# A Perceiver layer in fp32: Qk's last 64 channels on quarters of the PE array, weights issued by SP, the first group's q products in one slot, more filler products at the end

## The reference, cut to what matters

```python
def layer(x, ctx):                       # x (128, 32, 256), ctx (128, 257, 192)
    h = layernorm(x)
    q = (h @ Wq).heads(8, 64); k = (ctx @ Wk).heads(8, 64); v = (ctx @ Wv).heads(8, 64)
    x = x + softmax(q @ k.T * 64**-0.5) @ v @ Wo + bo          # cross attention
    h = layernorm(x) * ln_g + ln_b
    w = sigmoid(h @ Wx @ Ww + bw); k, v, r = h @ Wk2, h @ Wv2, sigmoid(h @ Wr2)
    # 4 heads of 64, over 32 steps: state = (1 - w) * state + k v^T;  out = r^T state
    x = x + out @ Wo2
    h = layernorm(x)
    return x + gelu(h @ U1 @ V1 + b1) @ U2 @ V2 + b2
```

## Time and profile before

| | before |
|---|---|
| median of 3 runs | 1028.94 us (1028.15 to 1028.95) |
| the profiled execution, its own time | 1036.5 us |
| its span | 1034.7 us |
| PE busy | 996.9 us, 96% of the span |
| ACT busy | 594.6 us, 57% |
| DVE busy | 503.5 us, 49% |
| POOL busy | 205.8 us, 20% |
| DMA | 79.03 MB, mean 76 GB/s |

### The profile page before, as it was taken

How to read it: one execution, slowest core, us unless ns; L and a number is a source line. 1 busy time by engine, 2 the same in 40 slices (tenths; PEclk the granted TensorE clock), 3 DMA queues, 4 the chain that set the end, 5 groups by cost and what they waited for, 6 DMA issues and landing times.

```text
span 1034.7 us, 21348 instructions
## 1 busy us (share of the span) xinstructions
PE 996.9 (96%) x8318; PEld 806.6 (78%) x8318; DVE 503.5 (49%) x1156; ACT 594.6 (57%) x1418; POOL 205.8 (20%) x356
## 2 busy tenths in 40 slices
PE   3799999999999999999999999999999999999987
PEld 3477888787888878788887878888887888887775
DVE  4444546363554536355453735545373554436152
ACT  2354637557574755758475675847467584746331
POOL 0010303113040312204031220403122040313130
PEclk9899999999999999999999999999999999999799
DMA  8233221222322222232212222222222322212000
GB/s 283 62 98 96 85 83 56 73 75 76 93 69 90 56 78 70 76 93 72 86 57 82 66 76 92 78 82 61 78 66 76 93 72 77 66 63 66 1 11 21
DMA packets 58002, 79.03 MB, mean 76 GB/s; under 512 B 10288, under 2 KB 39856, under 8 KB 57904
## 3 DMA queue, kind: packets, MB, share of 16 engines
q1 hardware_dynamic: 54304, 72.71, 23.2%
q10 hardware_dynamic: 3600, 4.96, 1.4%
HBM read 73.18 MB, written 4.46 MB: 75 GB/s over the span
## 4 chain that ended last, share of the span: by engine, by line
PE 66%; DVE 13%; ACT 12%; issue 4%; POOL 2%; ACTq 1%; SPq 1%; DMA 0%; POOLq 0%; DVEq 0%
PE gb L324 12%; PE scores L369 8%; PE scores L372 6%; PE gb L431 6%; PE gb L491 5%; PE acc L398 5%; PE ptp L381 4%; PE acc L394 4%; DVE inv L837 3%; PE acc L399 3%; ACT probs L603 3%; PE gb L540 3%; DVE probs L747 2%; ACT hid L668 2%; DVE nmax L740 2%
## 5 line engine op out<-in xcount | busy, mean ns | idle before, releaser
L603 ACT ACTIVATE probs<-scores,nmax 128x257 f32<-128x257 f32 x256 | 119.2, 472 | 171.4 <-DVE nmax L740 171.2
L740 DVE TENSOR_REDUCE nmax<-scores 128x2 f32<-128x514 f32 x128 | 88.6, 692 | 226.0 <-PE scores L372 226.0
L933 POOL TENSOR_TENSOR ptm<-probs,head 128x32 f32<-128x32 f32 x128 | 33.1, 259 | 601.9 <-DVE probs L747 601.9
L369 PE MATMUL scores<-raw_t,qk 128*128 128x257 f32 x512 | 134.0, 385 | 1.7 <-ACT qk L638 1.2
L369 PEld LDWEIGHTS scores<-raw_t,qk 128*128 128x128 f32 x512 | 88.1, 192 | 9.4 <-issue 1.6
L372 PE MATMUL scores<-raw_t,qk 64*128 64x257 f32 x512 | 91.2, 433 | 0.0
L747 DVE TENSOR_TENSOR probs<-probs,rinv 128x514 f32<-128x514 f32 x128 | 88.9, 695 | 4.4
L398 PE MATMUL acc<-pt,raw_n 128*128 128x256 f32 x256 | 90.0, 433 | 0.0
L381 PE MATMUL ptp<-ident,probs 128*128 128x128 f32 x512 | 79.0, 277 | 8.1 <-DVE probs L747 6.8
L394 PEld LDWEIGHTS acc<-pt,raw_n 128*64 128x64 f32 x1024 | 56.0, 137 | 37.0 <-issue 28.6
L394 PE MATMUL acc<-pt,raw_n 128*64 128x128 f32 x1024 | 83.5, 284 | 1.1 <-ACT pt L608 1.1
(11 more groups left out here) (140 smaller groups left out, 2356.8 us busy)
## 6 DMA issues: line engine op xcount, KB each, us to landing
raw_t<-in_ctx_t SPq DMA_DIRECT2D x128, 258.0 KB, 2.9
raw_n<-in_ctx_n SPq DMA_DIRECT2D x128, 192.0 KB, 2.4
xin<-in_x SPq DMA_DIRECT2D x16, 256.0 KB, 2.8
xb<-in_x SPq DMA_DIRECT2D x16, 256.0 KB, 2.8
vsp<-tail_values SPq DMA_DIRECT2D x256, 2.0 KB
out<-ob SPq DMA_DIRECT2D x16, 256.0 KB, 2.2
qk<-in_wq ACTq DMA_DIRECT2D x1, 512.0 KB, 4.5
wk<-in_wk SPq DMA_DIRECT2D x1, 512.0 KB, 5.4
```

The costliest lines, as they stand in the source:

```text
L369: mm(scores[:, r, 0:L], w[:, 0, b, r * P:(r + 1) * P], x[:, 0, 0:L], start=True, stop=False)
L603: go(probs[n % 2][:, r, 0:L], scores[:, r, 0:L], ACT.Exp, bias=nmax[:, r:r + 1], accum_out=rsum[:, r:r + 1]).then_inc(s["exp_ready"], 1)
L740: v_.tensor_reduce(nmax[:], scores[:, :, 0:L], AX.X, ALU.max, negate=True)\
```

## The change

**Qk.** `qk_wide(j, g)` (steps Qa0, Qa1) makes channels 0-127 of four heads (pairs p = j and j + 2) with four products of 64 rows and 128 columns of the array. `qk_rest(g)` (step Qb) makes channels 128-191 of all eight heads with eight products on 64 x 64 quarters of the array, into two banks. So a group has three Qk steps and six copies by ACT. `wk` is no longer padded (384 KB instead of 512). `qk` is 384 columns for each batch.

**Slots.** Qa0 in slot 3, Qa1 in slot 5, Qb in slot 6, none in slot 4; q2 and q1 change places (slots 2 and 3), and q3 goes from slot 5 to slot 4. Group 0 has its own table `BEGINNING`, with the four q steps in slot 2.

**The start.** The fifteen weight loads are issued by SP, ahead of the context tiles of batches 1 and 2. ACT does an Exp of two columns behind its small loads, waits for `xn0` and issues the load of x of group 1 itself. POOL waits for the weights only in `residual(0)`. The raw copy of wq is kept in `khat` instead of `qk[1]`, so DVE clears `khat` only after wq is split.

**The end.** `BUSY` has 5 fillers instead of 2 after XT2 of the last group, and 3 instead of 1 after its O2.

```diff
-FILL1 = [["Sq", "Qf", "WV"], ["O2"], [], ["Qk0"], ["Qk2"], ["Qk4", "H0"], ["Qk6"], ["Sp", "H2"]]
-FILL2 = [[], ["Y3", "Y1", "XT"], ["q0", "q1", "Y2", "XT2"], ["z", "q2", "XT3"], ["k", "Pf"], ["q3", "r"], ["v"],
+FILL1 = [["Sq", "Qf", "WV"], ["O2"], [], ["Qa0"], [], ["Qa1", "H0"], ["Qb"], ["Sp", "H2"]]
+FILL2 = [[], ["Y3", "Y1", "XT"], ["q0", "q2", "Y2", "XT2"], ["z", "q1", "XT3"], ["q3", "k", "Pf"], ["r"], ["v"],
          ["TP"]]
+BEGINNING = {1: ["XT"], 2: ["q0", "q2", "q1", "q3"], 3: ["Qa0"], 5: ["Qa1"], 6: ["Qb"]}
-BUSY = {("Y2", OLD): 4, ("XT2", NEXT): 2, ("H2", OLD): 2, ("Y3", OLD): 1, ("O2", NEXT): 1, ("Y2", NEXT): 9,
+BUSY = {("Y2", OLD): 4, ("XT2", NEXT): 5, ("H2", OLD): 2, ("Y3", OLD): 1, ("O2", NEXT): 3, ("Y2", NEXT): 9,
         ("XT3", NEXT): 1, ("Pf", NEXT): 1, ("H2", NEXT): 3, ("Qf", NEXT): 1}
...
+    if i == FIRST:
+        return [[(n, 0) for n in BEGINNING.get(b, [])], []]
...
-        wk = sb("wk", [P, 4, 256])
+        wk = sb("wk", [P, 4, C])
-        qk = [sb(f"qk{i}", [P, 2, G, 256]) for i in range(2)]
+        qk = [sb(f"qk{i}", [P, G, 256 + P]) for i in range(2)]
...
             load_t(0)
             load_n(0)
+            for dst, src in WEIGHTS:
+                sp.dma_start(dst, src).then_inc(wb_in, 16)
             for n in range(1, RING):
                 load_t(n)
                 load_n(n)
-            load_x(1)
             load_x(2)
...
+            def qk_wide(j, g):
+                even, odd = tile(f"Qa{j}e", g), tile(f"Qa{j}o", g)
+                drained(f"q{j}", g)
+                drained(f"q{j + 2}", g)
...
+                for k in range(2):
+                    p = j + 2 * k
+                    last_even = mm(even[:, k], wk[0:64, p, 0:P], qs[0:64, p], start=True, stop=True)
+                    last_odd = mm(odd[:, k], wk[64:128, p, 0:P], qs[64:128, p], start=True, stop=True)
...
+            def qk_rest(g):
+                even, odd = tile("Qbe", g), tile("Qbo", g)
+                for j in range(2):
+                    for k in range(2):
+                        p, half = j + 2 * k, slice(64 * k, 64 * k + 64)
+                        last_even = mm(even[half, j], wk[0:64, p, P:C], qs[0:64, p], start=True, stop=True)
+                        last_odd = mm(odd[half, j], wk[64:128, p, P:C], qs[64:128, p], start=True, stop=True)
...
-                    mm(scores[:, r, 0:L], w[:, 0, b, r * P:(r + 1) * P], x[:, 0, 0:L], start=True, stop=False)
+                    mm(scores[:, r, 0:L], w[:, b, r * P:(r + 1) * P], x[:, 0, 0:L], start=True, stop=False)
...
-                    mm(scores[:, r, 0:L], w[half, 1, b, r * P:(r + 1) * P], x[half, 1, 0:L], start=False,
+                    mm(scores[:, r, 0:L], w[half, b, 2 * P:3 * P], x[half, 1, 0:L], start=False,
...
-            for dst, src in WEIGHTS:
-                act.dma_start(dst, src).then_inc(wb_in, 16)
+            act.wait_ge(s["half_ready"], 1)
+            go(warm[:], half[:], ACT.Exp)
+            act.wait_ge(s["xn0_ready"], 1)
+            act.dma_start(xin[:], x_v[1]).then_inc(x_in, 16)
...
             def constants():
+                dve.wait_ge(s["wq_ready"], 1)
...
             def residual(g):
+                if g == 0:
+                    pool.wait_ge(wb_in, W_B)
...
             pool.wait_ge(small_in, W_S)
-            pool.wait_ge(wb_in, W_B)
```

More of the change, by code:

```diff
@@ L52 @@
           (NG + 1, 7): [("H2", NEXT), ("Qf", NEXT), ("Y3", NEXT)]}
-BUSY = {("Y2", OLD): 4, ("XT2", NEXT): 2, ("H2", OLD): 2, ("Y3", OLD): 1, ("O2", NEXT): 1, ("Y2", NEXT): 9,
+BEGINNING = {1: ["XT"], 2: ["q0", "q2", "q1", "q3"], 3: ["Qa0"], 5: ["Qa1"], 6: ["Qb"]}
+BUSY = {("Y2", OLD): 4, ("XT2", NEXT): 5, ("H2", OLD): 2, ("Y3", OLD): 1, ("O2", NEXT): 3, ("Y2", NEXT): 9,
         ("XT3", NEXT): 1, ("Pf", NEXT): 1, ("H2", NEXT): 3, ("Qf", NEXT): 1}
 TILES = {"WV": ["WV0", "WV1"]}
-for pair in ("Qk0 Qk1", "Qk2 Qk3", "Qk4 Qk5", "Qk6 Qk7", "H0 H1", "H2 H3"):
+for pair in ("H0 H1", "H2 H3"):
     TILES[pair.split()[0]] = pair.split()
+TILES.update({n: [n + "e", n + "o"] for n in ("Qa0", "Qa1", "Qb")})
 TILES.update({"Sp": ["S0", "S1"], "Sq": ["S2", "S3"]})
@@ L61 @@
 SHIFT.update({f"q{p}": PREP for p in range(4)})
-SHIFT.update({f"Qk{h}": PREP for h in range(H)})
+SHIFT.update({n: PREP for n in ("Qa0", "Qa1", "Qb")})
 SHIFT.update({n: POST for n in "WV Y1 XT2 z k r v Sp".split()})
@@ L166, in build @@
         ve, rstd, half = sb("ve", [P, 3, 2]), sb("rstd", [P, 3, 2]), sb("half", [P, 2])
+        warm = sb("warm", [P, 2])
         o_h, o_l = (sb(n, [P, 4, T], F32R) for n in ("o_h", "o_l"))
@@ L345, in q @@
                 done(f"q{p}", g, last)
[L347 to L351, removed]
-                    pe.wait_ge(wk_in, 16)
[L353 to L357, removed]
-                done(f"Qk{h + 1}", g, last_odd)
+            def qk_wide(j, g):
+                even, odd = tile(f"Qa{j}e", g), tile(f"Qa{j}o", g)
+                drained(f"q{j}", g)
+                drained(f"q{j + 2}", g)
+                if g == 0 and j == 0:
+                    pe.wait_ge(wk_in, 16)
+                for k in range(2):
+                    p = j + 2 * k
+                    last_even = mm(even[:, k], wk[0:64, p, 0:P], qs[0:64, p], start=True, stop=True)
+                    last_odd = mm(odd[:, k], wk[64:128, p, 0:P], qs[64:128, p], start=True, stop=True)
+                done(f"Qa{j}e", g, last_even)
+                done(f"Qa{j}o", g, last_odd)
+            def qk_rest(g):
[5 more added lines that the diff above has]
+                        last_odd = mm(odd[half, j], wk[64:128, p, P:C], qs[64:128, p], start=True, stop=True)
+                done("Qbe", g, last_even)
+                done("Qbo", g, last_odd)
             def score(n):
@@ L363, in score @@
                 if b == 0:
-                    drained("Qk7", g)
+                    drained("Qbo", g)
                 if n > 0:
@@ L557, in _ @@
                 steps[f"q{i}"] = lambda g, i=i: q(i, g)
-                steps[f"Qk{2 * i}"] = lambda g, i=i: qk_heads(2 * i, g)
             steps["Sp"], steps["Sq"] = lambda g: s_tiles(0, g), lambda g: s_tiles(1, g)
+            for j in range(2):
+                steps[f"Qa{j}"] = lambda g, j=j: qk_wide(j, g)
+            steps["Qb"] = qk_rest
             for i in (0, 2):
@@ L1062 @@
     wk = np.asarray(L0_xattn_Wk).T.reshape(H // 2, P, C).transpose(1, 0, 2)
-    wk = np.ascontiguousarray(np.concatenate([wk, wk[:, :, P:]], 2))
+    wk = np.ascontiguousarray(wk)
     wv = np.asarray(L0_xattn_Wv).reshape(C, H, DH)
```

18 lines of the change are left out of this document (11 added, 7 removed).

## The result

| | before | after |
|---|---|---|
| median, runs beside each other | 1028.95 us (1028.15 to 1033.03, 4 runs) | 1019.09 us (1018.98 to 1019.17, 4 runs) |
| ratio after / before | | 0.9896, 95% interval 0.987 to 0.9922 |
| the profiled execution, its own time | 1036.5 us | 1019.17 us |
| its span | 1034.7 us | 1017.4 us |
| PE busy | 996.9 us | 981.4 us |

A forecast was written before the change was run, and what follows sets the result against it. PE was taken as bound, with ACT's and DVE's chain setting slots 4 to 7 in rounds 2 to 14. Terms 7.3 + 0.85 - 0.1 + 3.5 = 11.5 us gave 1017.4 us, range 1010.5 to 1022.

The forecast's parts named there:

- Qk's products: Qk steps on PE: Qb takes 0.86 us, its extra shape costs 0.1, PE has 0.75 us less per group.
- The rounds: Rounds 2 to 14, slots 4 to 7: q3's copy leaves ACT's chain, 0.27 us per round, 3.5 us in all.
- The start: Program start: first q product at 11.05, scores of batch 0 at 20.9 instead of 28.19, 7.3 us gained.
- the two ends: Load of x of group 1: landing about 12 us costs nothing, about 22.4 costs 1.3 us; nothing was taken.
- Round 0: No Qk step ahead of `pv(4)` in slot 4, so SP's loads start earlier: 0.85 us gained.
- Round 1: DVE's chain hides slots 4 and 5, slot 6 pays for the extra shape: 0.1 us lost.
- Fillers: Fillers after XT2 and O2 of the last group lie in PE's waits: nothing gained or lost.
- it stands 7.6 above the median, which I carry over: Whole time: profiled execution 1036.5 lies 7.6 us above the median; the same excess was assumed for the change.
- rival B: PE's clock, late stretch at 1.2 GHz: without it 1010.4 us; with a second, or only in runs after, 1024.4; 8% each.

The follow-up runs named there:

- h0_dve_late: The change with Gelu steps H0 and H2 later and DVE's `pr` and `cf` behind slot 5's probabilities: 1009.81 us, ratio 0.9801.
- qb_twice: The change with every product of Qb made twice, sixteen instead of eight: 1021.29 us, ratio 0.9888.
- start_only: The kernel before with only the change's edits of the start, Qk as before: 1023.2 us, ratio 0.9933.
- q3_only: The kernel before with q3 moved from slot 5 to slot 4 and nothing else: 1033.81 us, ratio 1.0021.
- the second profile of the kernel before: The kernel before, unchanged, profiled again among the experiments: profiled execution 1028.09 us, median 1033.01 us.
- rounds_only: The change with the old start, keeping the new Qk steps, slots and fillers: 1025.54 us, ratio 0.9939.
- dve_late: The change with DVE's `pr` and `cf` behind slot 5's probabilities, H0 and H2 unmoved: 1016.45 us, ratio 0.9853.
- old_busy: The change with the old fillers of the last group, 2 after XT2 and 1 after O2: 1019.17 us, ratio 0.9879.
- h0_fill: The change with H0 and H2 later and three fillers in the last slot of round 15: 1015.45 us, ratio 0.9845.

## Why the prediction was right, and where it was off

*Qk's products: right.* Qb takes 0.86 us for eight products, as taken from the attention output's row. From slot 6's last scores to the first products of `pv` it takes 1.66 us where nothing waits (402.31 to 403.97 in `h0_dve_late`), and Qa1 in the same place of slot 5 takes 1.50 (396.44 to 397.94), so the extra shape costs 0.16 and not 0.1. For four row tiles the Trainium skill (TensorE: Matmul & The Clock Gate, Measured speedup vs the span model) gives 3.07 times. By it, as an estimate, Qb would take 1.1 us; for quarters in fp32 with 256 columns this trace shows the full factor, as four passes start every 0.21 us. In a round a slower Qb would have been nearly hidden, since by `qb_twice` even twice the work cost it 0.08 us. Outside these rounds it lies more in the open: the same 0.87 us cost about 3 us in the whole, so the extra 0.24 would have cost some 0.8 by proportion, near the 0.7 of the prediction.

*The rounds: right, in size a quarter low.* Forecast 0.27 per round by the copy of q3, measured 0.32 (60.20 to 59.88); the chain of DVE and ACT gave 0.28 of it (18.09 to 17.81). The other 0.04 is within what `start_only` moved the period (0.07) without touching the rounds. Round 14 gained 0.53 (0.5 forecast). From round 1 to 14 the table shows 4.4 us, 3.5 were forecast. PE's wait is 0.64 (0.72 forecast), but half of it stands ahead of `pv(6)`: with Qb done early PE runs into ACT's copy of the transposes there, which stands behind the Gelus as well. What the prediction gave no weight is that the move needs two edits at once: by `q3_only` the copy's 0.27 turns into a loss of 0.28 if Qk2 stays in slot 4. By these readings the 0.75 us that PE saves per group buys little by itself in these rounds; it makes the room for q3.

*The start: right.* First q product 11.08 (11.05), scores of batch 0 20.82 (20.9). x of group 1 was issued at 8.40 on ACT's queue and landed 6.8 us later, at 15.2; DVE's statistics took it at 16.15 and waited for nothing. That is between the two ends, 12 and 22.4. Two DMA issues, at 8.12 and at 8.40 us (KB, us from issue to landing), and what the queues of SP (q1) and ACT (q10) moved from 10 to 11 us (packets, MB, share of the engines):

```profile
qk<-in_wo SPq DMA_DIRECT2D x1, 256.0 KB, 8.8
xin<-in_x ACTq DMA_DIRECT2D x1, 256.0 KB, 6.8
...
q1 hardware_dynamic: 148, 0.40, 99.9%
q10 hardware_dynamic: 148, 0.00, 8.3%
```

The weight above it, of the same size, was issued by SP 0.3 us ahead of x and landed 1.7 us behind it. The Trainium skill (DMA: Bandwidth & Descriptors, Queues, rings and completion order) says that an engine takes the queues with work in turn. This trace agrees: from 10 to 11 us both queues moved 148 packets, SP's full ones and ACT's tiny ones. But ACT's queue was not otherwise empty, as the prediction had it: the last of its small loads, `vecs` of 4 KB issued at 5.04, landed only at 12.5, and x behind it. So x came at 15.2 and not at 12; no run tried it without the small loads. The gain was 7.4 against the first profile and 6.8 against the second, in which PE's pace rose sooner.

*Round 0: right.* From slot 0 to the scores behind the late tile it takes 39.69 us in the second profile of the kernel before and 39.68 in `start_only`, neither with a stretch at 1.2 GHz there. In `rounds_only`, also without such a stretch, it takes 38.86, 0.83 less (0.85 forecast). With the change it takes 40.51 with one of 3.4 us, in which PE is busy throughout; 1.7 off that gives 38.8. SP's loads remain in the chain of waits:

```profile
52.97 0.33 SPq L251
...
62.93 2.90 DMA raw_t<-in_ctx_t
...
65.87 1.13 PE scores L388 x4
```

But PE's own wait for the last tile, 0.49 and 0.52 us in the two profiles of the kernel before, is gone: the scores at 65.87 have no idle time ahead of them. PE and the tile now arrive together, so there is no free work left there.

*Round 1: right in direction.* From those scores to slot 7 of round 1 it takes 50.27 us, 0.12 more than in the first profile and 0.29 more than in the second, where 0.1 was forecast. DVE is the chain there; `dve_late` shows that by shortening it.

*Fillers: right,* nothing (`old_busy`).

*The step that failed: "it stands 7.6 above the median, which I carry over".* The excess was put on the clock correctly, but subtracting it from both kernels alike supposes that the change spends as little time at 1.2 GHz as the median run of the kernel before. It does not. The kernel before had 3.4 us at 1.2 GHz in one profile and 23.9 in the other, and its runs spread over 10 us; the change had the same three stretches of 3.4 us in both of its profiles and a clock of 0.994 or 0.995 in all ten runs, which lie within 1 us. Against the execution of the kernel before with one such stretch the terms give about 12.0 us (forecast 11.5), and two stretches take 3.4 back. That is rival B in its mild form ("one only in the runs after"), at half of its price.

That the time came out only 1.7 us off is partly luck. The rounds gave 0.9 more than forecast (4.4, not 3.5) and the start 0.5 less (6.8, not 7.3), and the kernel before's median beside the change, 1028.95, lay 0.9 above its execution with one stretch. By profile against profile the gain is 8.9 us, not 9.9.

What stays open is why the clock falls where it does. In `h0_fill` and `old_busy` fillers, put in or left out, took no stretch of a profile away.

## What to carry to other kernels

Before a step is moved off an engine's chain, look at what the slot that takes it must give up: the same move gained 0.32 us a round with a step taken out of that slot, and lost 0.28 without. When a chain is shortened, name the next one behind it and its distance; here ACT's, DVE's and PE's lay 0.13 and 0.30 us apart, and only the edits to both together brought 0.43. Take a profile of an execution near the median before its excess is carried over, or a second one, and look at the mean granted clock of every run: from round 2 on the periods repeat to 0.05 us while the total moves by 10.

## What the hardware showed that was not expected

The same kernel ran at 1028.1 and at 1036.5 us with the same periods in every round from 2 to 15; the difference lies in how long the granted clock was at 1.2 GHz at two places. The prediction set the long stretch beside PE's waits ahead of it. These waits, from PE's timeline of the first profile,

```profile
957.22 0.66 PE L394 MATMUL acc<-pt,raw_n 128*64 128x128 f32 x8 [0.91 <-ACT pt L608]
...
962.26 2.40 PE L491 MATMUL gb<-rhat,khat 64*128 64x32 f32 x32 [1.12 <-POOL rhat L983]
```

and from that of the second,

```profile
953.32 0.66 PE L394 MATMUL acc<-pt,raw_n 128*64 128x128 f32 x8 [0.91 <-ACT pt L608]
...
958.37 1.98 PE L491 MATMUL gb<-rhat,khat 64*128 64x32 f32 x32 [1.12 <-POOL rhat L983]
```

are the same to the last digit, and only the first was followed by 13.7 us at 1.2 GHz. The waits alone don't decide it.

A small operation of DVE can take several times its usual time when POOL has an instruction running, because it then ends only when POOL's does. `cf`, a copy of 128 x 48, takes 0.73 us in round 6 of the change, beside a product of POOL:

```profile
401.82 0.77 POOL L977 TENSOR_TENSOR khat<-kt,su 128x256 f32<-128x256 f32 x1
401.92 0.73 DVE L873 COPY cf<-tot 128x48 f32<-128x48 f32 x1
```

In rounds 14 and 15, where POOL is idle at that moment, it takes 0.20 us (at 880.64 and 937.43). In every other round of the change that has it, it ends 0.05 to 0.07 us behind POOL's instruction. `h0_dve_late` fits: `cf` stands beside a short instruction of POOL there and takes 0.23 us, ending 0.05 behind it, while the product of 128 x 16 behind it (L877), 0.19 us in the change with POOL idle, takes 0.63 beside another of POOL and ends 0.05 behind that one. And `wb` (L874), which in most rounds starts just as one instruction of POOL ends and takes 0.22 us, takes 0.80 in three rounds of the change and ends 0.08 behind POOL's next. Moving `pr` and `cf` therefore moved the delay from one operation to another and did not remove it; what counts is whether the chain of waits runs over it.
